# A recommendation tower: one TensorE signal per looked-up table, layer blocks drained in pairs, one output row

## The reference

```python
e = jnp.stack([tbl_0[ids[:, 0]], ..., tbl_25[ids[:, 25]]], axis=1)
sd = jnp.einsum('bfd,bd->bf', sparse_values, dense_features)
ss = jnp.einsum('bfd,bgd->bfg', sparse_values, sparse_values)
pairs = ss[:, iu, ju]
z = jnp.concatenate([dense_features, sd, pairs], axis=1)
h = jnp.concatenate([z, r_dense_features], axis=1)
h = jnp.maximum(h @ W_top1 + b_top1, 0.0)      # 607 x 512
h = jnp.maximum(h @ W_top2 + b_top2, 0.0)      # 512 x 256
y = h @ W_top3                                 # 256 x 1
```

## Time and profile before

| | us |
|---|---|
| runs | 557.14, 558.03, 558.73 |
| median | 558.03 |
| profiled execution | 554.1 |
| its span | 552.2 |
| TensorE busy (of the span) | 375.6 (68%) |
| VectorE busy | 231.4 (42%) |
| ScalarE busy | 174.7 (32%) |
| GpSimd busy | 277.3 (50%) |

### The profile page before, as it was taken

One profiled execution on the slowest core, in us unless ns is written; L12 is line 12 of the kernel. 1 busy time (PEld: TensorE's weight loads), 2 busy tenths in 40 slices (PEclk: granted clock), 3 DMA queues, 4 the chain that ended last, 5 costly groups with the idle time before them and its releaser, 6 DMA issues.

```text
span 552.2 us, 12229 instructions
## 1 busy us (share of the span) xinstructions
PE 375.6 (68%) x5424; PEld 294.6 (53%) x5424; DVE 231.4 (42%) x579; ACT 174.7 (32%) x221; POOL 277.3 (50%) x297
## 2 busy tenths in 40 slices
PE   2650587426379959955489859954559859975697
PEld 0430455315267648745367647743448648864576
DVE  5610687414144553532244443632226535505500
ACT  1400345313132343421142333421215324443122
POOL 7777467563416656753516756663416666610000
PEclk9985599667579979976579969965569978996699
DMA  8522263110102112211101112211101111100000
GB/s 201 142 53 52 67 198 89 40 49 23 40 8 53 44 38 53 66 35 37 40 10 52 44 38 52 63 43 30 27 20 40 43 43 49 43 18 4 4 0 1
DMA packets 11596, 26.93 MB, mean 49 GB/s; under 512 B 5033, under 2 KB 5161, under 8 KB 11409
## 3 DMA queue, kind: packets, MB, share of 16 engines
q0 software_dynamic: 9216, 18.89, 13.4%
q1 hardware_dynamic: 2328, 7.27, 4.9%
HBM read 26.14 MB, written 0.01 MB: 47 GB/s over the span
## 4 chain that ended last, share of the span: by engine, by line
PE 62%; issue 21%; ACT 7%; another core or an unknown queue 7%; DMA 2%; POOL 1%; DVE 1%
PE sum_bank L410 22%; PE vec_bank L436 12%; PE work_bank L462 8%; PE vec_bank L426 6%; PE work_bank L472 5%; ACT vecT L316 3%; PE work_bank L458 3%; PE work_bank L481 2%; ACT vecT L310 2%; PE work_bank L450 2%; PE id_bank L396 1%; DMA rows<-in_tbl,ids_all 1%; ACT parts L296 1%; ACT late L342 1%
## 5 line engine op out<-in xcount | busy, mean ns | idle before, releaser
L221 POOL DMA_INDIRECT rows<-in_tbl,ids_all x288 | 274.6, 953 | 207.7 <-PE vec_bank L426 86.5
L253 DVE TENSOR_TENSOR onehot<-id_bank,row_f 125x1024 fp32r<-125x1024 f32 x128 | 151.6, 1220 | 170.6 <-PE sum_bank L410 72.8
L410 PE MATMUL sum_bank<-onehot,parts 125*128 125x512 f32 x512 | 166.0, 459 | 4.2 <-DVE onehot L253 4.2
L436 PE MATMUL vec_bank<-vecT 128*26 128x26 f32 x4096 | 68.7, 215 | 81.4 <-issue 73.7
L410 PEld LDWEIGHTS sum_bank<-onehot,parts 125*128 125x128 f32 x512 | 103.1, 213 | 30.8 <-issue 12.2
L316 ACT COPY vecT<-vec_bank 128x512 f32<-128x512 f32 x72 | 85.3, 1200 | 80.7 <-remote 49.0
L436 PEld LDWEIGHTS vec_bank<-vecT 128*26 128x26 f32 x4096 | 56.4, 131 | 96.4 <-issue 85.0
L264 DVE STREAM_TRANSPOSE late<-late 128x832 f32<-128x832 f32 x16 | 28.7, 1793 | 113.6 <-ACT late L325 113.6
L426 PE MATMUL vec_bank<-ident,rows 128*128 128x128 f32 x288 | 52.1, 314 | 10.6 <-DMA rows<-in_tbl,ids_all 3.8
L325 ACT COPY late<-vec_bank 128x416 f32<-128x416 f32 x32 | 16.2, 507 | 123.1 <-PE vec_bank L436 123.1
L426 PEld LDWEIGHTS vec_bank<-ident,rows 128*128 128x128 f32 x288 | 41.2, 162 | 23.9 <-issue 11.7
(11 more groups left out here) (23 smaller groups left out, 99.2 us busy)
## 6 DMA issues: line engine op xcount, KB each, us to landing
rows<-in_tbl,ids_all POOLq DMA_INDIRECT x288
late<-in_tbl SPq DMA_DIRECT2D x8, 480.0 KB
w_all<-in_weights SPq DMA_DIRECT2D x1, 1540.0 KB
xT<-in_dense_t SPq DMA_DIRECT2D x4, 256.0 KB
late<-in_weights SPq DMA_DIRECT2D x1, 256.0 KB
ids_all<-in_ids SPq DMA_DIRECT2D x1, 208.0 KB, 3.0
late<-in_tbl SPq DMA_DIRECT2D x8, 20.0 KB
vecT<-in_ids_t SPq DMA_DIRECT2D x1, 64.0 KB
```

Of the source, the lines that this page charges most:

```text
L221: nc.gpsimd.indirect_dma_start(rows[:, g % ROWS_RING, n, t, :], None, tables[f], bass.IndirectOffsetOnAxis(ids_all[:, TD * d + t, f:f + 1], 0)
L253: nc.vector.tensor_tensor(onehot[:, use % RING, :, :], bass.AP(got.tensor, got.offset, [got.ap[0], [0, PW], [1, QS]]), bass.AP(numbers.ten ...
L410: last = nc.tensor.matmul(sum_bank[into % 2][:], parts[:, part, CH_AT[n] + c0 + c, :], onehot[:, use % RING, c, :], start=(p % PER == 0 an ...
L436: last = nc.tensor.matmul(vec_bank[into % 2][BL * j:BL * j + GC, i * GC:(i + 1) * GC], vecT[:, s, 0:GC], vecT[:, s, 1:VECS], start=True, s ...
```

## The change

- TensorE signals once per table (`table_done`), after its last pack, in place of after each pack and each spread. The same signal stands for three things: the sum is whole, the four packs are free, and the ids of the table after the next are spread, since that spread now comes ahead of the table's last pack.
- The one-hot ring has 8 packs, two tables. VectorE waits only at a table's first pack: for the whole table two before. The first two spreads have a signal of their own (`ids_spread`).
- All four turns of a quad come after pack 7 of the next.
- Two blocks of layer 1 share a bank (and the two of layer 2): one signal and one wait for both, two activations one behind the other.
- Layer 3 has the weights as the stationary side: 2 matmuls of 256 columns into one partition in place of 4 with one column. The output collects on two partitions, a half each, and is stored by two DMAs.

```diff
-    RING = 6
+    AHEAD = 2
+    RING = AHEAD * PER
...
+    MB = 512 // DS
     W1 = TD
-    W2 = W1 + M1
-    W3 = W2 + M2
+    W2 = W1 + M1 // MB
+    W3 = W2 + M2 // MB
...
-    TURN_AFTER = {RING - 1: [0, 1, 2], RING + 1: [3]}
+    TURN_AFTER = {RING - 1: [0, 1, 2, 3]}
...
+        lines = sb("lines", [65, BATCH], fp16)
+        idsT = lines[0:NH, :]
+        y_half = [lines[32 * (h + 1):32 * (h + 1) + 1, :].bitcast(fp32) for h in range(2)]
...
-            sp.dma_start(y.rearrange("(p t) o -> p (t o)", t=TILES), y_cols[:]).then_inc(y_stored, 16)
-            sp.wait_ge(y_stored, 16)
+            for h in range(2):
+                sp.dma_start(y.rearrange("(p h t) o -> h p (t o)", p=P, h=2)[h:h + 1],
+                             y_half[h].rearrange("o (p t) -> o p t", p=P)).then_inc(y_stored, 16)
+            sp.wait_ge(y_stored, 32)
...
-                    dve.wait_ge(id_filled, NH * q + n + 1)
-                if use >= RING:
-                    dve.wait_ge(pack_done, use - RING + 1)
+                    if NH * q + n < AHEAD:
+                        dve.wait_ge(ids_spread, n + 1)
+                    else:
+                        dve.wait_ge(table_done, NH * q + n - AHEAD + 1)
...
-                act.wait_ge(pack_done, PER * use + PER)
+                act.wait_ge(table_done, use + 1)
...
-            def drain_unit(d, at, m, h, b):
-                if d == 0 and at == W1 and m == 0:
+            def drain_units(d, at, m, h, b):
+                if d == 0 and at == W1 and m == MB - 1:
                     act.wait_ge(weights_loaded, 16)
-                use = NW * d + at + m
+                use = NW * d + at + m // MB
                 act.wait_ge(work_filled, use + 1)
-                nc.scalar.activation(h[:, m, :], work_bank[use % 2][:, 0:DS], ACT.Relu,
-                                     bias=b[:, m:m + 1]).then_inc(work_drained, 1)
+                for k in range(m - MB + 1, m + 1):
+                    last = nc.scalar.activation(h[:, k, :], work_bank[use % 2][:, k % MB * DS:(k % MB + 1) * DS],
+                                                ACT.Relu, bias=b[:, k:k + 1])
+                last.then_inc(work_drained, 1)
...
-                nc.scalar.copy(y_cols[:, TD * d:TD * (d + 1)], work_bank[use % 2][:, 0:TD]).then_inc(work_drained, 1)
+                t0 = TD * d % (TILES // 2)
+                nc.scalar.copy(y_half[2 * d // DUOS].rearrange("o (p t) -> o t p", p=P)[:, t0:t0 + TD, :],
+                               work_bank[use % 2][0:1, 0:DS].rearrange("o (t p) -> o t p", t=TD)
...
+                    if m % MB == MB - 1:
+                        drain_units(2 * q + d, W1, m, h1, b1_sb)
...
-                if q >= QUADS:
-                    return
-                if use >= 2:
-                    pe.wait_ge(pack_set, PER * (use - 1))
-                nc.tensor.matmul(id_bank[use % 2][:], pick[:, n, :],
-                                 idsT[:, q * QS:(q + 1) * QS], start=True, stop=True).then_inc(id_filled, 1)
+                return nc.tensor.matmul(id_bank[use % 2][:], pick[:, n, :],
+                                        idsT[:, q * QS:(q + 1) * QS], start=True, stop=True)
 
...
+                if p % PER == PER - 1 and into + AHEAD < NH * QUADS:
+                    spread_ids(into + AHEAD)
...
-                last.then_inc(pack_done, 1)
+                if p % PER == PER - 1:
+                    last.then_inc(table_done, 1)
...
             def layer1(d, m):
-                use = NW * d + W1 + m
-                free_work(use)
-                cols, out = slice(m * P, (m + 1) * P), work_bank[use % 2][:, 0:DS]
-                nc.tensor.matmul(out, w1x[:, cols], xT[:, d // 2 % 2, d % 2 * DS:(d % 2 + 1) * DS], start=True, stop=False)
+                use, at = NW * d + W1 + m // MB, m % MB * DS
+                if m % MB == 0:
+                    free_work(use)
+                cols, out = slice(m * P, (m + 1) * P), work_bank[use % 2][:, at:at + DS]
+                nc.tensor.matmul(out, w1x[:, cols], xT[:, d // 2 % 2, d % 2 * DS:(d % 2 + 1) * DS],
+                                 start=True, stop=False)
                 if m == 0:
                     pe.wait_ge(work_drained, NW * d + W1)
                 for b in range(KT):
                     last = nc.tensor.matmul(out, w1p[:, b, cols], pairsT[0:KP, b, :],
                                             start=False, stop=(b == KT - 1))
-                last.then_inc(work_filled, 1)
+                if m % MB == MB - 1:
+                    last.then_inc(work_filled, 1)
...
             def layer3(d):
                 use = NW * d + W3
                 pe.wait_ge(work_drained, use)
-                for t in range(TD):
-                    for b in range(M2):
-                        last = nc.tensor.matmul(work_bank[use % 2][:, t:t + 1], h2[:, b, t * P:(t + 1) * P],
-                                                w3_sb[:, b:b + 1], start=(b == 0), stop=(b == M2 - 1))
+                for b in range(M2):
+                    last = nc.tensor.matmul(work_bank[use % 2][0:1, 0:DS], w3_sb[:, b:b + 1], h2[:, b, :],
+                                            start=(b == 0), stop=(b == M2 - 1))
...
-            spread_ids(0)
-            spread_ids(1)
+            for use in range(AHEAD):
+                spread_ids(use).then_inc(ids_spread, 1)
...
-                    if p % PER == 1:
-                        spread_ids(NH * q + p // PER + 2)
```

20 lines of the change are left out of this document (10 added, 10 removed).

## The result

The changed kernel takes **568.42 us** (median of four runs, 563.94 to 570.80) beside 558.38 for the kernel before (four runs, 557.14 to 560.29). The ratio is 1.0167, 95% interval 1.0097 to 1.0237: **slower by 10 us** between the medians and by 9.3 by the ratio. The interval excludes no change and leaves open whether it is more than 2%. Forecast was 557.0, with 533 to 567 as the range. The profiled execution of the changed kernel is its quickest: 563.94 us with a span of 562.1, against 554.1 and 552.2 before.

What follows compares the result with a forecast made beforehand. The prediction took TensorE's signals queuing up while GpSimd streams gathers as the bound. Terms -3.5 + 1.8 - 1.5 + 0 + 2.2 = -1.0 us gave 553.1 profiled, 557.0 us as a median, range 533 to 567.

Steps and rivals of the forecast that it cites:

- What bounds the kernel: While GpSimd streams gathers, TensorE's signals queue up, most likely among its finished instructions; stalls of 6 to 25 us.
- First quad: First quad's lookups and dot products: fewer GpSimd pauses and up to 1.4 us at the restart, -3.5 us (0 to -6.8).
- give-back: First quad: TensorE's lookup gain, 4 to 6 us ahead, is lost in dot products that crawl until GpSimd stops.
- Quads 1 to 3: Their lookups: VectorE has slack, nothing new waits, the stall before layer 3 stays; terms +1.8 and -1.5 us.
- activations' +1.8: Before layer 3 in quads 1 to 3: a second activation after the stall, +0.3 to +0.48 us, six times.
- shorter queue's -1.5: Quads 1 to 3: fewer queue entries elsewhere, -1.5 us, taken between 0 and one whole stall of 6.4.
- Layer 3: Four records of 256 columns replace eight of one column: 0 us after a stall, bounds -0.9 and 0.
- Tail: End of kernel: two-activation drains +1.6, last copy +0.3, second store +0.35 and +0.5; taken as +2.2 us (+1 to +4).
- Signals are the load: Rival, whole kernel: signal entries cost the queue several times plain ones; halving them gives -20 to -40, near 530; chance 0.17.
- Longer streams: Rival, quads 1 to 3: GpSimd streams one more group, TensorE waits longer before layer 3; about 565 us; chance 0.20.
- No gain in the first quad: Rival, first quad: GpSimd pauses as often as before, tail and activations stay, +2.5: 560.5 us; chance 0.08.
- The fixed price per signal: Rival, TensorE: each semaphore increment costs 26.3 ns, serialized; 150 fewer give an estimated 3.9 us less, 553; chance 0.05.

Runs made afterwards that it cites:

- e4: The changed kernel with 126 TensorE signals put back that nobody waits for: 559.44 us, ratio 1.0108 to the kernel before.
- e1: The kernel before with only the signals per table, ring of eight packs and moved turns and spreads: 552.59 us beside 553.46, ratio 0.9979.
- e2: The kernel before with only the paired drains of layers 1 and 2: 556.63 us, ratio 1.0034.
- e12: The kernel before with only the signals, ring of eight and turns, repeated on the faster kind of chip: +0.2 us (-1.6 to +2.0).
- e5: The changed kernel again, unaltered, on the faster kind of chip: 441.95 us beside 435.33 for the kernel before, ratio 1.0136.
- e18: The changed kernel with the output of before (layer 3 in columns, one copy, one store), faster kind of chip: +3.1 us over the kernel before.
- e9: The kernel before itself, unaltered, run for a trace on the faster kind of chip: 434.75 us, ratio 1.0015.
- e8: The kernel before with GpSimd waiting after each group of four gathers until it has landed: 538.99 us beside 435.33, ratio 1.2395.
- e15: The kernel before with GpSimd waiting after each eight gathers until they have landed: 475.80 us, ratio 1.1004.

## Why the prediction was wrong, step by step

The forecast was -1.0 us, and +9.3 (5.4 to 13) was measured. By the stages of the two profiled executions, q0 came 4.3 us over its term, quads 1 to 3 the same (+4.6 for +0.3, which e4's trace does not repeat), and the tail 2.1.

*What bounds the kernel* fits A as a reading of the trace: TensorE's signals late while GpSimd streams, the queue most likely one of finished instructions. e4 agrees with the last point (126 more signals, no price), and the single matmuls 2.8 us apart at 47 to 57 with nothing to wait for are the earlier trace rows again in the lookups. That GpSimd is the cause was argued and not shown: it rests on the stage tables of A and B, since the run without gathers never fell on A.

*First quad, -3.5* (bounds 0 and -6.8): **this step failed.** It came to +0.8. Its give-back was right (5.6 us gained in the lookups, 6.4 lost in the dot products, free at 124.44). What failed is the rest: 2.8 us that GpSimd's own pauses were to lose (5.3 to 2.5), and 0.7 at the restart. Behind 61 us GpSimd paused for 2.0, 1.6 and 2.3 us before, and for 1.7 and 2.5 after: one pause went, two stayed, and the 44 gathers took 43.1 us for 42.3, so its stretch ended only 0.6 us earlier. The restart came 1.1 us later behind that end and not up to 1.4 sooner. Over the whole kernel GpSimd's pauses are the same, 40.4 us in 16 before and 40.0 in 16 after,

```profile
POOL rows L221 <- remote: 40.4, 16, 5.9
```

```profile
POOL rows L225 <- remote: 40.0, 16, 5.4
```

and GpSimd is the engine that ends the crawl. q0 took 149.6, 149.5, 150.3 and 150.1 us in the traces of e1 to e4, with and without the signals. A gain for TensorE alone was no reason to take anything but 0.

*Quads 1 to 3:* "nothing new waits" was wrong. What it cost is not shown: this execution lost 4.6 us there, e4's trace nothing. The sum of the last table hangs on one late signal (17.1 us in four waits), in exchange for two of the six stalls before layer 3 (26.9 us down to 15.6). The activations' +1.8 and the shorter queue's -1.5 can't be found one by one; e1's -1.2 and e2's +1.9 allow both.

*Layer 3, 0* (bounds -0.9 and 0): about right on A, where five of six stood behind a stall (+0.07 there); at full clock, as on B, outside the bounds, +0.15 each time. I had priced the eight one-column records by a row at a stall (1.86 us at half clock) and halved layer 2 for the new form; at full clock the old form takes 0.81 and the halved layer 2 (0.95) was right. For a place without a stall the old form had to be put at full clock too.

*Tail, +2.2* (bounds +1 and +4): **mis-sized.** It came to 4.3, of which the rows above give 3.6. The drains were right (1.6, now 1.5). The copy was 0.44 for 0.3: an activation on 128 partitions was no bound for a copy that writes one partition with a stride. The stores were 1.3 for 0.85. The wait of the next duo for that copy (0.4) was missed: I had looked only at the end. Clock adds up to 1 us.

*The rivals.* "Signals are the load" fell with e4 and e12. "Longer streams" (565) came nearest in time but not in kind: no stream of q1 to q3 grew past twelve gathers. In the traces of e1 and e4 one stream in each of these quads did reach sixteen, and q1 to q3 took 356.4 and 359.2 us beside 359.9, so such a stream did not cost what the rival gave it. "No gain in the first quad" (560.5, 0.08) was what happened, with a tail 1.4 us dearer than priced. The fixed price per signal had 0.05; neither e1 (-1.2, -3.0 to +0.7) nor e12 (+0.2, -1.6 to +2.0), which take 126 signals away, shows a gain that needs it. By the Trainium skill ("TensorE: Matmul & The Clock Gate", The cost: per-tile semaphore tail) each increment adds 26.3 ns, an estimated 3.3 us for e4's 126. A gain of that size is outside both intervals, unless the ring or the turns cost as much; e4 and the changed kernel were not run on one chip together, so no run here tests that figure alone.

By its steps, then, without the gain in q0 and with the true tail the sum would have read +0 + 1.8 - 1.5 + 0.9 + 3.6 = 4.8, with layer 3's price of B. That lies within B's interval (4.4 to 7.4) and is half of A's first figure. The agreement is partly luck, since no row shows the +1.8 and the -1.5.

## What to carry to other kernels

Signals between engines are worth removing only where an engine waits for them and is the one that sets the end; here the lookups gained 5.6 us and GpSimd's gathers took it back in the next stage. Here a result copied to one partition and stored in two pieces was paid in full at the end of the kernel, where nothing covered it (1.7 us). Price the last copy, its stores and the neighbour that waits for the same bank from rows of that form. And before a stall is taken for the machine's nature, see whether another chip has it: the stage tables of two chips side by side showed where 120 us sit, which no trace of one chip could.

## What the runs showed of the hardware

- The kernel before took 553 to 558 us in two comparisons (one of them on the chip of e1 to e4) and 432 to 436 on the five chips of e5 to e18, at the same clock in its quiet stages. In the trace of the first kind signals of TensorE reach other engines more than 25 us late while GpSimd issues gathers; in that of the other kind (e9) no wait is put down to a late signal ("remote"), through 240 gathers in a row. That this is the whole of the 120 us was not tested on the first kind. What makes a chip the one or the other was not found.
- Single fp32 matmuls 2.8 us apart, with no wait in the rows, at 47 to 57 us in the changed kernel on the first kind.
- Four fp32 records of 256 columns with a one-column load take 0.96 us, eight records of one column with a full load 0.81 us, at full clock.
- On the second kind, pausing GpSimd for each group's landing costs 104 us of 435 (e8), and for every second group 44 (e15): the pause is paid by the transposes that wait for rows.
